# Residual sums by accumulating DMAs on pre-copied tensors, and projection stores issued by ACT

## The reference

```
x = x + 0.5 * ffn(layernorm(x))
x = x + attn(layernorm(x))
x = x + 0.5 * ffn(layernorm(x))

ffn(y):  h = relu(y @ W1 + b1); alpha = softmax(h @ W2 + b2)        # 8 experts
         out = sum_k alpha_k * U_k @ (V_k @ y)                      # rank 64 each
attn(u): z = layernorm(u) * gamma + beta; q, k, v = z @ qkv
         out = softmax(causal(q k^T / sqrt(2048))) @ v @ o_proj + u
```

## Time and profile before

| what | value |
|---|---|
| runs shown | 8167.17 and 8781.3 us, median 8474.24 us |
| profiled execution | 8178.52 us; span of its slowest core (7) 8177.0 us |
| spans of the eight cores | 8120.1 to 8177.0 us |
| PE busy | 6200.8 us, 76% |
| DVE, ACT, POOL busy | 1209.6, 630.9, 1627.9 us |
| moved by DMA | 486.47 MB, mean 59 GB/s |
| all of the HBM queues' packets | 14.3% (hardware queue) and 4.9% (software queue) of 16 engines' span |

### The profile page before, as it was taken

How to read it: one execution, slowest core, us unless ns; L and a number is a source line. 1 busy time by engine, 2 the same in 40 slices (tenths; PEclk the granted TensorE clock), 3 DMA queues, 4 the chain that set the end, 5 groups by cost and what they waited for, 6 DMA issues and landing times. The chain is left out here.

```text
span 8177.0 us, 86393 instructions; the slowest of 8 cores (8120.1 to 8177.0 us)
## 1 busy us (share of the span) xinstructions
PE 6200.8 (76%) x29108; PEld 3016.1 (37%) x29108; DVE 1209.6 (15%) x1414; ACT 630.9 (8%) x972; POOL 1627.9 (20%) x4076
## 2 busy tenths in 40 slices
PE   2898699216998899988887377356669993997898
PEld 2343343113333343433333133135634442433343
DVE  2112211441000000001111011100020003112212
ACT  1000100231000000000000000000010001000000
POOL 0450251001222222222221000022100000540450
PEclk7899799658989998998888678678879995998899
DMA  2113112211111111111111411311132223113112
GB/s 73 48 46 103 59 48 62 107 77 48 43 41 43 47 43 40 43 35 34 33 37 37 119 39 35 112 34 37 38 119 77 77 67 82 46 39 121 48 47 93
DMA packets 514020, 486.47 MB, mean 59 GB/s; under 512 B 212890, under 2 KB 460746, under 8 KB 490034
## 3 DMA queue, kind: packets, MB, share of 16 engines
q1 hardware_dynamic: 478770, 337.27, 14.3%
q0 software_dynamic: 34816, 143.69, 4.9%
HBM read 336.95 MB, written 143.82 MB: 59 GB/s over the span
## 5 line engine op out<-in xcount | busy, mean ns | idle before, releaser
L272 POOL CAST w1hi<-w1f 128x128 bf16<-128x128 f32 x1792 | 568.6, 317 | 2556.5 <-PE psA L666 1380.1
L666 PE MATMUL psA<-bigA_hi,w1hi 128*128 128x512 bf16 x3072 | 845.9, 401 | 218.8 <-DVE ht_lo L284 153.1
L666 PE MATMUL psA<-bigA_lo,w1hi 128*128 128x512 bf16 x3072 | 843.3, 400 | 0.0
L666 PE MATMUL psA<-bigA_hi,w1lo 128*128 128x512 bf16 x3072 | 825.0, 393 | 0.0
L274 POOL TENSOR_TENSOR w1lo<-w1f,w1hi 128x128 bf16<-128x128 f32 x1792 | 770.1, 430 | 264.7 <-POOL w1hi L272 7.0
L447 PE MATMUL psA<-bigA_hi,w1hi 128*128 128x512 bf16 x2048 | 613.3, 381 | 18.3 <-DVE bigA_lo L407 18.3
L447 PE MATMUL psA<-bigA_lo,w1hi 128*128 128x512 bf16 x2048 | 611.9, 380 | 0.0
L447 PE MATMUL psA<-bigA_hi,w1lo 128*128 128x512 bf16 x2048 | 611.8, 380 | 0.0
L666 PEld LDWEIGHTS psA<-bigA_hi,w1hi 128*128 128x128 bf16 x3072 | 307.7, 101 | 623.5 <-issue 328.6
L666 PEld LDWEIGHTS psA<-bigA_lo,w1hi 128*128 128x128 bf16 x3072 | 313.9, 102 | 404.5 <-issue 104.8
L284 DVE TENSOR_TENSOR ht_lo<-psA,ht_hi 128x256 bf16<-128x256 f32 (+1 forms) x160 | 127.6, 798 | 2225.5 <-ACT ht_hi L279 1578.0
(11 more groups left out here) (173 smaller groups left out, 5642.5 us busy)
## 6 DMA issues: line engine op xcount, KB each, us to landing
w1f<-W SPq DMA_DIRECT2D x1024, 64.0 KB, 1.9
w1f<-qkv SPq DMA_DIRECT2D x768, 64.0 KB, 1.8
xa<-x_scratch SPq DMA_DIRECT2D x32, 1024.0 KB, 4.8
xa<-x SPq DMA_DIRECT2D x16, 1024.0 KB, 5.7
x_scratch<-xa POOLq DMA_DIRECT2D x16, 1024.0 KB, 9.4
xp_scratch<-xa POOLq DMA_DIRECT2D x16, 1024.0 KB, 4.5
xa<-xp_scratch SPq DMA_DIRECT2D x16, 1024.0 KB, 5.0
out<-xa POOLq DMA_DIRECT2D x16, 1024.0 KB, 8.6
```

Source lines behind the costliest of these rows:

```text
L272: p.do("gpsimd", lambda e: e.tensor_copy(out=hi_ap, in_=src_ap), reads=src_bufs, writes=[hi_buf], inc="g")
L666: last = e.matmul(out=pa[:, n0:n1], lhsT=wop[:, ws * 128:(ws + 1) * 128], rhs=zop[:, di * S + n0:di * S + n1], start=(di == 0 and pi == 0) ...
```

## The change

Four residual sums leave the compute engines. At its start each of the phases 1, 2, 5 and 6 now copies its whole residual tensor, HBM to HBM, tile by tile (16 DMAs of 1 MB, issued by SP through `dma_in`), into the tensor that it will produce. The tiles' results are then added onto it by a DMA with `accum_op=ALU.add`, issued by POOL (`dma_acc`). All 16 copies name one buffer as written (`x1t`, `xpt`, `x2t`, `outt`), and each accumulating DMA names that buffer too. What the compute engines did for the sums changes: in phases 1 and 6 the second load of x is gone, and ACT instead of DVE scales the PSUM result by 0.5; in phase 2 the DVE addition L609 is gone, and what is accumulated is `ytile` itself, a single buffer; in phase 5 the load of the `xp_scratch` tile is gone and ACT instead of DVE moves the PSUM result. Apart from that, the stores of q, k and v are issued by ACT (`dma_out_hw`) instead of POOL. The unused lists `TRS` go away.

```
+    def dma_acc(dst_ap, src_ap, reads, writes=()):
+        sem = "stB_" + reads[0].name
+        return p.do("gpsimd", lambda e, d=dst_ap, s=src_ap: e.dma_start(out=d, in_=s, accum_op=ALU.add),
+                    reads=reads, writes=writes, inc=sem, n=16)
+
+    def dma_out_hw(dst_ap, src_ap, reads, writes=()):
+        sem = "shB_" + reads[0].name
+        return p.do("scalar", lambda e, d=dst_ap, s=src_ap: e.dma_start(out=d, in_=s),
+                    reads=reads, writes=writes, inc=sem, n=16)
...
-    def ffn_phase(src_h, dst_h, srcb, dstb):
+    def ffn_phase(src_h, dst_h, srcb, dstb, dtag):
         yTh, yTl = gb("bigA_hi"), gb("bigA_lo")
-        TRS = [psa(0, 128), psa(1024, 1152), psc(0, 128)]
+        dtile = gb(dtag)
+        for t_ in range(NT):
+            dma_in(dst_h[t_ * 128:(t_ + 1) * 128, :], src_h[t_ * 128:(t_ + 1) * 128, :],
+                   writes=[dtile], reads=[srcb])
...
-                xr = (ytile, ttile)[i % 2]
-                xrb = gb(("ytile", "ttile")[i % 2])
-                dma_in(xr[:], src_h[ti * 128:(ti + 1) * 128, :], writes=[xrb], reads=[srcb])
...
-                    p.do("vector", lambda e, pa=pa, dh=dh, xr=xr, ob=ob, DW=DW: e.scalar_tensor_tensor(
-                        out=ob[:, dh * DH:dh * DH + DW], in0=pa[:, 0:DW], scalar=0.5,
-                        in1=xr[:, dh * DH:dh * DH + DW], op0=ALU.mult, op1=ALU.add),
-                        reads=pab + [xrb], writes=[obb], inc="v")
-                dma_out(dst_h[ti * 128:(ti + 1) * 128, :], ob[:], reads=[obb], writes=[dstb])
+                    p.do("scalar", lambda e, pa=pa, dh=dh, ob=ob, DW=DW: e.activation(
+                        out=ob[:, dh * DH:dh * DH + DW], in_=pa[:, 0:DW], func=AF.Copy, scale=0.5),
+                        reads=pab, writes=[obb], inc="s")
+                dma_acc(dst_h[ti * 128:(ti + 1) * 128, :], ob[:], reads=[obb], writes=[dstb, dtile])
...
     def proj_phase():
+        xpt = gb("xpt")
+        for t_ in range(NT):
+            dma_in(xp_h[t_ * 128:(t_ + 1) * 128, :], x1_h[t_ * 128:(t_ + 1) * 128, :],
+                   writes=[xpt], reads=[gb("x1_h")])
...
-            p.do("vector", lambda e, xa=xa: e.tensor_tensor(out=xa[:], in0=xa[:], in1=ytile[:], op=ALU.add),
-                 reads=[gb("ytile")], writes=[xab], inc="v")
-            dma_out(xp_h[ti * 128:(ti + 1) * 128, :], xa[:], reads=[xab], writes=[gb("xp_h")])
+            dma_acc(xp_h[ti * 128:(ti + 1) * 128, :], ytile[:], reads=[gb("ytile")],
+                    writes=[gb("xp_h"), xpt])
...
-                dma_out(dst_hi[row:row + 128, :], hh[:, 0:S], reads=[hhb], writes=[gb("q_h") if do_ < NC else gb("k_h")])
+                dma_out_hw(dst_hi[row:row + 128, :], hh[:, 0:S], reads=[hhb], writes=[gb("q_h") if do_ < NC else gb("k_h")])
...
-            xa = (xa0, xa1)[i % 2]
-            xab = gb("xa%d" % (i % 2))
-            dma_in(xa[:], xp_h[i * 128:(i + 1) * 128, :], writes=[xab], reads=[gb("xp_h")])
...
+        x2t = gb("x2t")
+        for t_ in range(NT):
+            dma_in(x2_h[t_ * 128:(t_ + 1) * 128, :], xp_h[t_ * 128:(t_ + 1) * 128, :],
+                   writes=[x2t], reads=[gb("xp_h")])
         t_loaded = load_tile(0)
...
-                p.do("vector", lambda e, pa=pa, dh=dh, xa=xa, ob=ob, DH=DH, DW=DW: e.tensor_tensor(
-                    out=ob[:, dh * DH:dh * DH + DW], in0=pa[:, 0:DW], in1=xa[:, dh * DH:dh * DH + DW], op=ALU.add),
-                    reads=pab + [xab], writes=[obb], inc="v")
-            dma_out(x2_h[i * 128:(i + 1) * 128, :], ob[:], reads=[obb], writes=[gb("x2_h")])
+                p.do("scalar", lambda e, pa=pa, dh=dh, ob=ob, DH=DH, DW=DW: e.activation(
+                    out=ob[:, dh * DH:dh * DH + DW], in_=pa[:, 0:DW], func=AF.Identity),
+                    reads=pab, writes=[obb], inc="s")
+            dma_acc(x2_h[i * 128:(i + 1) * 128, :], ob[:], reads=[obb], writes=[gb("x2_h"), x2t])
```

More of the change, by code:

```diff
@@ L681, in proj_phase @@
                 split_hilo(pa[:, 0:S], pab, hh[:, 0:S], hhb, hl[:, 0:S], hlb)
-                dma_out(dst_hi[row:row + 128, :], hh[:, 0:S], reads=[hhb], writes=[gb("q_h") if do_ < NC else gb("k_h")])
-                dma_out(dst_lo[row:row + 128, :], hl[:, 0:S], reads=[hlb], writes=[gb("q_h") if do_ < NC else gb("k_h")])
+                dma_out_hw(dst_hi[row:row + 128, :], hh[:, 0:S], reads=[hhb], writes=[gb("q_h") if do_ < NC else gb("k_h")])
+                dma_out_hw(dst_lo[row:row + 128, :], hl[:, 0:S], reads=[hlb], writes=[gb("q_h") if do_ < NC else gb("k_h")])
             else:
@@ L700, in pend_v @@
                     vo_lo = bass.AP(v_lo_h.tensor, dv * 128, [[D, 128], [128 * D, NT], [1, 128]])
-                    dma_out(vo_hi, hh[:, 0:S], reads=[hhb], writes=[gb("v_h")])
-                    dma_out(vo_lo, hl[:, 0:S], reads=[hlb], writes=[gb("v_h")])
+                    dma_out_hw(vo_hi, hh[:, 0:S], reads=[hhb], writes=[gb("v_h")])
+                    dma_out_hw(vo_lo, hl[:, 0:S], reads=[hlb], writes=[gb("v_h")])
                 pend.append(pend_v)
@@ L920, in load_tile @@
                     dma_in(hbuf[:, c0 * 128:c1 * 128], ap_in, writes=[bb], reads=[gb("aot_h")])
-            xa = (xa0, xa1)[i % 2]
-            xab = gb("xa%d" % (i % 2))
-            dma_in(xa[:], xp_h[i * 128:(i + 1) * 128, :], writes=[xab], reads=[gb("xp_h")])
-            return ah, al, ahs, als, xa, xab
+            return ah, al, ahs, als, None, None
+        x2t = gb("x2t")
+        for t_ in range(NT):
+            dma_in(x2_h[t_ * 128:(t_ + 1) * 128, :], xp_h[t_ * 128:(t_ + 1) * 128, :],
+                   writes=[x2t], reads=[gb("xp_h")])
         t_loaded = load_tile(0)
@@ L970, in build @@
         if cut >= 2:
-            ffn_phase(x_h, x1_h, gb("x_in_h"), gb("x1_h"))
+            ffn_phase(x_h, x1_h, gb("x_in_h"), gb("x1_h"), "x1t")
     if "p2" in phases:
@@ L981, in build @@
         prep_vu()
-        ffn_phase(x2_h, out_h, gb("x2_h"), gb("out_hb"))
+        ffn_phase(x2_h, out_h, gb("x2_h"), gb("out_hb"), "outt")
     fin = [(s, p.cnt[s], 16) for s in p.cnt if s.startswith("stB_")]
```

## The result

| | before | after |
|---|---|---|
| median of the runs | 8707.64 us (10 runs) | 9146.07 us (11 runs) |
| lowest | 8148.82 us | 8518.71 us |
| profiled execution, span | 8178.52, 8177.0 us | 8538.03, 8536.5 us |
| PE, DVE, ACT, POOL busy | 6200.8, 1209.6, 630.9, 1627.9 us | 6145.7, 1057.0, 727.9, 1578.0 us |
| moved by DMA | 486.47 MB | 503.24 MB |

A forecast was written before the change was run, and what follows sets the result against it. No single engine bounds the whole: PE bounds the long matmul stretches, and the first load bounds each phase's start. Copies +444, accumulating DMAs +20 and the rest -1 give +463 us on 8177.0, so 8642 us; range 8480 to 8950.

The forecast's parts named there:

- Direction and place of the loss: Four phase starts: slower, chance 0.95; 16 chained copies on SP, engines idle: +115, +115, +113, +101 us.
- I take the middle, 7.2 us: Copies at the phase starts: price of one 1 MB copy, between bounds of 5.0 and 9.4 us.
- the 16.6 that I counted as covered: Copies: 2 us hidden by attention stores landing in output projection, 14.6 us by V and U preparation in last feed-forward.
- a fixed part and a transfer: Copies' lower bound: about 1.6 us fixed plus 3.3 us for the rest, 4.9 us per 1 MB.
- The sentence on the pair's limit: Copies: 716 GB/s per core pair gives 5.9 us transfer, 7.5 us with fixed part, sum 19 us higher; unproven.
- The accumulating DMA: Residual stores: 9.0 us each, fitting the 10.36 us tile pace of the last matmul stage, so PE doesn't feel it.
- The five ends: Two feed-forward group turns, ends of first feed-forward, output projection and kernel, where something waits for the store: together +20 us.
- The rival of slow accumulation: Last matmul stage: accumulating DMA becomes the bound, from about 10.1 us each; at 18.8 us, 8937 us total; chance 0.21.
- to free POOL gives 0: Projections: matmuls wait for DVE, not POOL, so moving q, k and v stores to ACT gains 0 us.
- DVE's addition (L609): Projections: removing it gains 0, its 2.3 us lying in a gap; if wrong, 37 us.
- I forecast against that: Base of the forecast: profiled execution beside the lower run, 8167.17 us, not the median 8474.24; +5.7%.
- The sum itself: Whole kernel: 444 us copies, +20 store ends, -1 evacuation, together +463 us; likeliest case's chance 0.62.

The follow-up runs named there:

- experiments 2 to 4: Changed kernel with copies unchained (8508.23 us lowest); with 8 chained 2 MB copies per place (8703.46 us); unchained in 4 KB pieces (8522.67 us).
- experiment 5: Kernel before, with q, k and v stores issued by ACT and the loads of k unchained, one buffer per chunk: lowest 8046.54 us.
- experiment 6: Changed kernel with each tile's copy issued beside running work, into its own buffer, instead of 16 at each phase's start: lowest 8189.36 us.
- experiment 8: experiment 6 with plain stores instead of accumulating DMAs, residual additions left out: 8102.6 us; also kernel before with only ACT's q, k, v stores: 8103.76 us.
- experiment 3: Changed kernel with eight chained copies of 2 MB in each of the four places instead of sixteen of 1 MB: 8703.46 us, single execution.

## Why the prediction was right or wrong

- **Direction and place of the loss: right.** Four runs of 16 copies on SP with nothing beside them; three of the places are paid in full and in the last feed-forward the preparation of V and U covers some of it. The forecast of 101 us there came out as 90, of 113 in the output projection as 100.5, of 115 twice as 106.3 and 104.4.
- **The step "I take the middle, 7.2 us": too high.** The four places cost 401.4 us. With the 16.6 that I counted as covered, that is 418 / 64 = 6.5 us a copy; 43 us of the forecast too much. The number was near, but its model was not, and that the middle of two bounds came within 0.7 us is luck. I had built the price of a fixed part and a transfer; experiments 2 to 4 show a price of little but traffic: 2 MB read and written in all, at about 325 GB/s, gives 6.5 us whether copies are chained or not, large or small. The sentence on the pair's limit had the right idea, as experiment 5 shows: an estimated 5.9 us at the 716 GB/s named there, 6.5 measured; the 1.6 us of fixed part that it added took it past, to 7.5.
- **The accumulating DMA: right where it counts, its size a bit high.** 7.9 us to landing against the 9.0 taken, hidden at 10.36 us a tile. The five ends read +3.5 us (end of the first feed-forward), +4.8 and +3.2 at the two turns (from the store's issue to DVE, each against the same turn before), +4.5 at the end of the output projection (9.8 us from the last issue to SP's next load, 5.3 before), and +3.6 at the kernel's end (9.2 us from the last issue to the span's end, 5.6 before): 19.6 us, the forecast's 20. The rival of slow accumulation did not occur, but experiment 6 shows how near it was: when copies burst into that stage, each DMA takes 8.3 us and more, and the chain is the bound.
- **The step "to free POOL gives 0": wrong, by 10 us.** I looked for who waits for POOL among the waits of L666, and the projections' matmuls take 4 to 6 us less all the same; why is open. And I did not look at the stretch between the last matmul and the first load of k, where 5.7 us are gained. Its last rows before:

```profile
4480.55 1.15 POOL L250 DMA_DIRECT2D v_hi<-ht_hi  x1 [10.67 <-ACT ht_hi L279]
4486.11 1.15 POOL L250 DMA_DIRECT2D v_lo<-ht_lo  x1 [4.41 <-DMA v_hi<-ht_hi]
4491.72 0.33 SPq L245 DMA_DIRECT2D bigA_hi<-k_hi  x1
```

and after:

```profile
4637.96 0.37 ACTq L260 DMA_DIRECT2D v_hi<-ht_hi  x1
4642.00 0.37 ACTq L260 DMA_DIRECT2D v_lo<-ht_lo  x1
4643.16 5.28 SPq L245 DMA_DIRECT2D bigA_hi<-k_hi  x2
```

The second store follows the first after 4.0 us instead of 5.6. And SP's first load of the next phase comes 1.2 us after the issue of the last store instead of 5.6, while no store of `v_lo` lands in under 3.8 us: with ACT's store the end of the block is not held until it has landed, with POOL's it is. (The loads of v name `v_h` and wait for it by themselves.)
- **DVE's addition (L609): right.** The projections' 16 tiles took 420-421 us before and 421-422 after.
- **The step "I forecast against that", the lower run: this put the time outside the range.** The 463 us were added to the level of the lower run shown, 8178.5 us. The measured time is the median of eleven runs, 9146.07, and eight of them lie at 8719 us and above; the median of before's own ten runs is 8707.64, not the level of its profiled execution. Added to that median, the same 463 us would give 9171, 25 us from the measured; so near a hit would be luck, since the eight runs spread over 865 us. Nothing in a profile says where in the spread of the runs a median falls. The two runs shown lay 614 us apart, and a range for the median had to be as wide above the profiled level as they were. What lowers the clock in those runs stays open.
- **The sum itself: 463 us forecast, about 410 by the stages.** By its terms the change costs 401 + 20 - 1 - 10 = 410 us. Between the profiled executions there are 360 only, since before's had a pair of cores at a lowered clock for part of the projections. Two cores of that execution, the same window, first core 7 and then core 5:

```profile
2254.00:2368.00 114.00, 104.34 (x384) 42.40 (x384) 4.58 (x2) 3.86 (x3) 25.10 (x68) 0.78 0.11 37
...
2254.00:2368.00 114.00, 104.45 (x471) 46.48 (x470) 4.58 (x2) 3.75 (x2) 30.27 (x84) 0.97 0.13 42
```

Core 7 has a granted clock of 0.78 and 384 matmuls, core 5 has 0.97 and 471. That cost core 7 some 53 us (2535 us of projection matmuls, 2482 elsewhere), and 8178.5 + 410 - 53 = 8535 is the profiled 8538. The profile of before showed this, had I set the cores' rows beside each other.

## What to carry to other kernels

The residual loads stood beside matmuls here and nothing waited long for them; the copies at the phases' starts were paid in full: before work is moved into DMAs, ask where each transfer would stand and whether anything runs there (400 us here for transfers that cost nothing beside running work, experiment 8). To tell a chain's waits from a traffic limit, read the DMA share with the GB/s and count both directions: loads at half share and 165 GB/s doubled when the chain was cut, copies at the same two numbers did not. And put the cores' stages side by side before one execution is taken as the base.

## What the runs showed of the hardware that was not expected

- HBM-to-HBM copies on all eight cores move 151 to 170 GB/s a core, chained or not, in pieces of 64 KB or 4 KB, as DMAs of 1 or 2 MB; the DMA engines' busy share is 0.5 or 1.0 at the same rate, so that share alone says nothing of what is left. The limit is shared by two cores (0 and 1, 4 and 5, 6 and 7 show it): a copy of 2 MB took 8.3 to 8.7 us while the other core of the pair made none, and 12.5 to 12.9 while it did (experiment 3's trace).
- An accumulating DMA of 1 MB from SBUF lands after 7.9 us and, back to back, comes every 8.3 to 9.1 us; a plain store takes 4.3. Its issue holds POOL for 0.85 us, a plain one's for 0.53. Beside a burst of 8 copies the first one took 24 to 30 us.
- One pair of cores can run at a lowered granted clock for part of a long matmul stretch while the other six do not, in the same execution: 0.78 against 0.96 to 0.97 in the profile of before, 0.81 against 1.00 in that of experiment 6. Both lie between the clock's two levels, 0.5 and 1 (1.2 and 2.4 GHz), and the windows do not tell whether it stood there or went to and fro. It happened in the profiles of before (three pairs, in different stages) and of experiment 6, and hardly in that of after. What sets it off stays open.
